# Softmax pieces of a five-layer graph attention kernel, two to a group instead of one, and the message lag cut from twelve groups to ten

## The reference

```python
def hgt_conv(x, src, dst, ntype, etype, Wk, Wq, Wv, Wa, pri, att, msg, skip):
    k = typed_linear(x, ntype, Wk).reshape(n, H, HD)
    q = typed_linear(x, ntype, Wq).reshape(n, H, HD)
    v = typed_linear(x, ntype, Wv).reshape(n, H, HD)
    kw = typed_linear_heads(k[src], etype, att)
    a = jnp.sum(kw * q[dst], axis=-1) * pri[:, etype].T / np.float32(np.sqrt(HD))
    amax = jax.ops.segment_max(a, dst, num_segments=n)
    ae = jnp.exp(a - amax[dst])
    w = ae / jax.ops.segment_sum(ae, dst, num_segments=n)[dst]
    m = typed_linear_heads(v[src], etype, msg) * w[:, :, None]
    h = jax.ops.segment_sum(m, dst, num_segments=n).reshape(n, D)
    h = typed_linear(h, ntype, Wa)
    alpha = jax.nn.sigmoid(skip)[ntype][:, None]
    return h * alpha + x * (jnp.float32(1.0) - alpha)
for l in range(5):
    h = hgt_conv(h, ..., Wk[l], Wq[l], Wv[l], Wa[l], rel_pri[l], rel_att[l], rel_msg[l], skip[l])
out = layernorm(x + h)
```

## Time and profile before

| | |
|---|---|
| median of 3 runs | 9909.23 us (9865.0 to 9917.3) |
| span of the profiled execution | 9921.5 us |
| PE, PEld busy | 5554.4 us, 4735.9 us |
| DVE, ACT, POOL busy | 4643.5 us, 4066.5 us, 4557.4 us |
| mean granted TensorE clock, share of full speed | 0.740 |
| indirect gathers (L443) | 4160, 957 ns each |

### The profile page before, as it was taken

The page is one execution under the profiler, slowest core; times in us unless marked ns, Lnnn a source line. Parts: engine busy times, 40 slices in busy tenths (PEclk is TensorE's granted clock), DMA queues, the critical chain, the costliest instruction groups (busy, mean ns, idle before and its releaser), DMA issues.

```text
span 9921.5 us, 147395 instructions
## 1 busy us (share of the span) xinstructions
PE 5554.4 (56%) x33354; PEld 4735.9 (48%) x33355; DVE 4643.5 (47%) x12764; ACT 4066.5 (41%) x10084; POOL 4557.4 (46%) x4797
## 2 busy tenths in 40 slices
PE   5654545586554555955555559445454594555554
PEld 3544444464444444744444447344444573444443
DVE  5254545532555555235554552355555523555555
ACT  1244444432444444324444443344444433444442
POOL 0345555433455554335555542445555424555553
PEclk9866676797677666977666679767767796676667
DMA  2322222213222221232222213222222132222221
GB/s 69 144 62 70 70 71 70 68 70 125 69 71 72 71 72 56 100 107 72 69 72 72 69 45 124 93 69 71 70 70 71 37 140 83 73 74 73 73 76 36
DMA packets 272656, 761.00 MB, mean 77 GB/s; under 512 B 87871, under 2 KB 104356, under 8 KB 271908
## 3 DMA queue, kind: packets, MB, share of 16 engines
q0 software_dynamic: 199680, 545.53, 19.2%
q1 hardware_dynamic: 72228, 208.51, 5.4%
HBM read 557.87 MB, written 195.88 MB: 76 GB/s over the span
## 4 chain that ended last, share of the span: by engine, by line
PE 31%; another core or an unknown queue 25%; DVEq 16%; issue 12%; DVE 10%; POOLq 3%; ACT 2%; ACTq 1%; DMA 0%; POOL 0%; SPq 0%
PE ps L535 6%; PE ps L627 6%; DVEq L1061 5%; DVEq L1051 5%; PE ps L643 4%; PE ps L648 4%; PE ps L552 3%; POOLq L459 3%; DVEq L228 2%; PE ps L555 2%; PE ps L588 1%; PE ps L642 1%; DVE prod L1045 1%; DVE wmsg L1025 1%
## 5 line engine op out<-in xcount | busy, mean ns | idle before, releaser
L443 POOL DMA_INDIRECT rows<-table,idx_now x4160 | 3981.4, 957 | 3529.5 <-DVE wmsg L1029 1878.9
L642 PE MATMUL ps<-zeros,identb 128*128 128x132 bf16 x2080 | 555.0, 267 | 3189.9 <-DVE wmsg L1029 2780.9
L704 ACT ACTIVATE prod<-iota_n,dloc 128x128 bf16<-128x128 f32 x6240 | 1988.9, 389 | 106.0 <-issue 78.7
L642 PEld LDWEIGHTS ps<-zeros,identb 128*128 128x128 bf16 x2080 | 242.1, 116 | 3353.3 <-issue 3171.5
L1045 DVE TENSOR_TENSOR prod<-ps,rows 128x512 f32<-128x512 f32 x1040 | 715.5, 688 | 2352.6 <-remote 1820.4
L709 ACT ACTIVATE ohf<-prod,ones 128x512 f32<-128x512 bf16 x1040 | 750.5, 722 | 2326.4 <-remote 1887.0
L627 PE MATMUL ps<-qn,ohT 128*128 x8320 | 1583.6, 350 | 67.8 <-issue 62.7
L627 PEld LDWEIGHTS ps<-qn,ohT 128*128 128x128 f32 x8320 | 1407.3, 255 | 135.9 <-issue 129.7
L643 PE MATMUL ps<-wmsg,ohf 128*128 128x132 f32 x4160 | 1267.6, 398 | 0.0
L648 PE MATMUL ps<-wmsg,ohf 128*128 128x132 f32 x4160 | 1090.9, 355 | 0.0
L588 PE MATMUL ps<-identb,oh 128*128 128x128 bf16 x4160 | 531.8, 268 | 730.4 <-ACT ohT L721 358.8
(11 more groups left out here) (162 smaller groups left out, 6391.4 us busy)
## 6 DMA issues: line engine op xcount, KB each, us to landing
table<-rows SPq DMA_DIRECT2D x245, 768.0 KB, 3.2
rows<-table,idx_now POOLq DMA_INDIRECT x4160
out<-h SPq DMA_DIRECT2D x1, 3072.0 KB
wk<-in_L_gnn_Wk SPq DMA_DIRECT2D x20, 48.0 KB
wq<-in_L_gnn_Wq SPq DMA_DIRECT2D x20, 48.0 KB
wv<-in_L_gnn_Wv SPq DMA_DIRECT2D x20, 48.0 KB
wa<-in_L_gnn_Wa SPq DMA_DIRECT2D x20, 48.0 KB
attw<-in_L_gnn_rel_att SPq DMA_DIRECT2D x20, 24.0 KB
```

The lines of the kernel that those rows point to most:

```text
L443: pool.indirect_dma_start(out=rows[:, slot, j, :], out_offset=None, in_=table, in_offset=bass.IndirectOffsetOnAxis(ap=idx_now[:, half, c:c ...
L642: pe.matmul(bank[:, AW:2 * AW], identb[:], zeros[:], start=True, stop=True)
L704: act.activation(squares[:, turn % 2, j * P:(j + 1) * P], iota_n[:], ACT.Square, bias=dloc[:, at(4 * q + j)], scale=-1.0)
```

## The change

`LAG` goes from `BQ + 4` to `BQ + 2`. Of the four pieces, 0 and 1 now stand one after the other at slot 0, and 2 and 3 at slot 1, on PE and DVE at the end of the position as before. ACT's exponentials move from slot 3 to slot 1, with the wait for piece 2 that is now of the same position. Message work of group a moves from position a + 12 to a + 10, so that the weighting that POOL waits for comes two positions sooner and each layer's edge phase ends at position 218 instead of 220. The ring stays at 16 groups.

```diff
-LAG = BQ + 4
+LAG = BQ + 2
...
-        def piece(slot, n):
+        def pieces(slot, n):
...
-            return (None, None) if k > 3 or is_first(n) or beyond(n - 1, BLOCKS) else (k, n - 1)
+            return () if k > 1 or is_first(n) or beyond(n - 1, BLOCKS) else ((2 * k, n - 1), (2 * k + 1, n - 1))
...
-                    k, m = piece(slot, n)
-                    if k is not None:
+                    for k, m in pieces(slot, n):
                         softmax_piece(k, m, 1 - slot // BQ)
...
-                    k, m = piece(slot, n)
-                    if k == 3:
+                    for m in [m for k, m in pieces(slot, n) if k == 3]:
                         act.wait_ge(s_smd, l * (SM * BLOCKS) + SM * m + 3)
...
-                    k, m = piece(slot, n)
-                    if k is not None:
+                    for k, m in pieces(slot, n):
                         softmax_piece(k, m, 1 - slot // BQ)
```

## The result

The kernel after takes 10445.99 us (median of 4 runs, 10445.14 to 10447.37) against 9904.95 us before on the same chip: 1.0546 times as long, 95% interval 1.0521 to 1.0571. The forecast was 10315 us, with a range of 9750 to 10640. The sign, the mechanism and some three quarters of the size were as forecast; of a loss of 522 us between the two profiled spans (10443.3 against 9921.5) the sum had 406.

A forecast was written before the change was run, and what follows sets the result against it. Bound by waits: PE's completions reach other engines late while POOL issues gathers back to back. 120 blocks x 3.0 + 46 at the ends = 406 us on the 9921.5 span, less 12 for the median: 10315 us, range 9750 to 10640.

The forecast's parts named there:

- The rule to issue a DMA early and wait late: Rival: remote waits are late gathers, so two groups more of lead shorten them; some 9210 us, chance 0.05.
- (1) The lead at zero: POOL's gathers may run six groups ahead of the product instead of four; this hides nothing, cost zero.
- (2) Pieces 0 and 1: With both in one position, DVE idles from piece 0's end until PE's part of piece 1 comes: 0.6 us.
- (3) Pieces 2 and 3: With both in one position, DVE waits through ACT's exponentials and PE's transposes: 1.7 us, plus 0.5 us for queued ACT work.
- The chain behind ACT's wait: ACT's message one-hot and copy queue behind its wait, delaying PE's next query product: 0.5 us shows, bounds 0 and 3.
- (4) Where the bursts fall: POOL's gather bursts give two long product waits in the six quick positions: +3.0 us a block, bounds -3 and +5.6.
- The walk: Step through one new block from the weighting at slot 2: two bursts of three groups, next such weighting at 64.7 us.
- The fifth taken off: Cut of 2.6 us from the two long product waits, since remote waits average 7.5 us, not 12; gives 62.1 us a block.
- the walk as it stood: Rival: both long product waits uncut, or worse; +5.6 us a block, 10630 us and above, chance 0.06.
- (5) Ends: Ends of each layer's edge phase: POOL restarts two positions sooner, pairs cost there, tail shorter; +9 us a layer, +46 in all.
- come apart: Rival: quick positions' weightings come 5 us apart or more, the second long wait goes; 56 us a block, 9595 us, chance 0.14.
- The even case: Rival: waits of pieces 0 to 3 shrink by the pairs' 2.8 us; block stays 59.1 us, 9955 us, chance 0.15.

The follow-up runs named there:

- few_before: Kernel before, with only the first of each group's four gathers issued from group 16 of each layer on; 7365.77 us, 0.7429 times the kernel before.
- lead4: Kernel after, with POOL held back by two more weightings so it runs four groups ahead as before; 9890.31 us, 0.9983 times the kernel before.
- half_again: Kernel after, with every gather moving half rows (512 bytes) from group 16 of each layer on; 10439.96 us, 1.0546 times the kernel before.
- few_after: Kernel after, with only the first of each group's four gathers issued from group 16 of each layer on; 7821.65 us, 0.7888 times the kernel before.
- pairs_lag12: Kernel after with LAG back at BQ + 4, so only the pairing of the pieces is left; 9922.58 us, 1.0012 times the kernel before.

## Why the prediction was right, and where its sum was off

**What bounds.** That remote waits are PE's completions held up by gathers, and not late rows, stands: the rows had landed long before, few_before loses the waits with the gathers, lead4 gains with a shorter lead, half_again keeps them with half the bytes. (Groups 2 to 4 of the first stretch had been issued 33 to 70 us before their products, not all some 60; that changes nothing.) That a wait lasts until 3.4 us after the burst's last gather holds in the block walked through, and not in all, as lead4 shows. Of the Trainium skill's rule that a DMA never contends with a compute engine ("SBUF — State Buffer", Who interferes with whom), half_again shows that the bytes indeed do not matter; the rest of these waits it does not foresee. The rule to issue a DMA early and wait late ("DMA: Bandwidth & Descriptors", Rules for kernel authors) was priced at 9210 us; here it gained nothing, with 10446, because no landing was left to hide.

**(1) The lead at zero** was right as a cover: the profile puts 2 waits, 1.0 us in all, down to a landing of rows. But the lead is also what places the bursts, and lead4 shows that there it is worth 556 us.

**(2) Pieces 0 and 1** and **(3) Pieces 2 and 3.** The hand-overs last as forecast: 0.58 us in the row of L974 (0.6 forecast) and 1.61 in that of L1002 (1.7). But part of them had been paid before. In the 24 blocks, few_after against few_before, the waits at L974 grew by 0.4 us a block and those at L1002 by 1.1, together 1.5 where the sum had 2.3. The chain behind ACT's wait, put at 0.5 us with bounds of 0 and 3, is the mis-sized term: the product's waits, 2.84 us at slot 2, grew by 2.2 us a block. Together that is 3.7 by the waits and 3.6 by the windows, where the sum had 2.8. Beside the bursts even the sign at L974 was off: all its waits fell from 136 us before, most of it remote, to 73 after; those at L1002 grew by 1.0 us each of 130 times, 1.5 forecast.

**(4) Where the bursts fall.** The walk was close. From the weighting at slot 2 (end at 2636.33) the first burst began at 3.9 (walk: 4.7) and had its last start at 18.1 (18.5); slot 4's product came at 21.2 (21.9); the second burst ran from 25.2 to 39.5 (25.9 to 39.7), slot 7's product came at 42.6 (43.1), slot 0 weighted at 45.8 (46.2), and the next block's weighting at slot 2 ended at 62.7 (64.7), mainly because the pairs took 16.9 us instead of 18.5. The next block takes 65.1 us, and they go on by turns; the mean is 63.8, so the walk was 0.9 us too long.

**The fifth taken off** the two long waits, 2.6 us, is where the block's +3.0 went wrong against a measured +4.1 (+4.5 without the ends). Its ground was the mean of 244 remote waits, 7.5 us. That mean puts long waits together with the short ones behind a single group, and says nothing on how often a long one is cut. The block before did get cut now and then; the block after does not. Yet the total came out nearer with it: the walk as it stood gave 10630, 184 us too much, and the forecast is 131 too little. Its +5.6 was too large even against the +4.5 of the steady blocks, its pairs above all, and the whole phase takes in the short last ones. So the fifth, without a ground, offset other errors; that is luck.

The second ground for +3.0, that (2) and (3) alone came to 2.8, was no ground. pairs_lag12 has the same pairs and costs 0.1%: beside bursts such a price is paid or not according to where the next burst falls. Two numbers from different causes happened to be near each other.

**(5) Ends**: +46 forecast, some 30 measured.

**The rivals.** The bursts did not come apart. The even case is what pairs_lag12 and lead4 measured, so it was right for the pairing and wrong for the lead that came with it.

## What to carry to other kernels

When one engine's bursts hold up another's results, price a change by where the bursts fall, by walking through one period with the trace's own durations, and check the walk against a second block; an average over unlike waits is no correction to it. In these runs latency saved or added was mostly absorbed by the burst beside it, so a longer lead, a shorter chain and a paired step can each be worth nothing, or several per cent, according to phase. Before tuning such a phase, see whether the disturbance is there on another chip.

## What the runs showed of the hardware that I had not expected

- On one chip, PE's completions are held up for up to some 30 us (the longest remote wait of the product: 28.7 in the kernel after, 30.6 in lead4) beside back-to-back indirect gathers, and on another they are not: 4 against 15 products in the first 85 us, 9908 against 7933 us for the kernel before, 10392 against 7898 for the same variant of the kernel after.
- The landings of the gathers' rows are told in time while PE's completions are not: the rows of the product at 2565.91 had been told of 30 us before, PE's word came at 2565.88.
- Halving the bytes of each gather in the loop (546 to 294 MB in all) left the time within 0.1% (10444 against 10440 us).
- One more wait in the issuing engine made the kernel 7% faster on the first chip (10444 to 9721 us).
